# Narrow attention of layers two and three: maxima split and output normalised on GpSimd, masks one step ahead, query rows through DRAM

## The reference

```python
# layer two: positions and a mask
scores = jnp.einsum('bhqd,bhkd->bhqk', Q, K) * scale
scores = scores - slopes[None, :, None, None] * dist[:, None, :, :]
scores = jnp.where(mask[:, None, :, :] == 0, -jnp.inf, scores)
m = jnp.max(scores, axis=-1, keepdims=True)
e = jnp.exp(scores - m)
attn = e / (1.0 + jnp.sum(e, axis=-1, keepdims=True))
out = jnp.einsum('bhqk,bhkd->bhqd', attn, V)          # then @ W_o.T
# layer three: biases, a fixed mask and a key padding, plain softmax
energy = jnp.einsum('bhse,bhke->bhsk', qh, kh) * scale
energy = jnp.where(keep, energy, neg)
attn = jax.nn.softmax(energy, axis=-1)
x = x + jnp.tanh(g_xattn[n]) * attention(_layernorm(x), ctx, ctx, ...)
```

## Time and profile before

| | |
|---|---|
| median of 3 runs | 1532.38 us (1531.8 to 1533.9) |
| profiled execution | 1531.62 us, span 1529.8 us |
| busy: PE, PEld | 1339.7 us (88%), 743.4 us (49%) |
| busy: DVE, ACT, POOL | 1051.6 us (69%), 795.8 us (52%), 678.7 us (44%) |
| layer two attention | from 798.1 us to 1080 us of the span |
| layer three attention | from 1233.3 us to 1507 us of the span |

### The profile page before, as it was taken

The page is one execution under the profiler, slowest core; times in us unless marked ns, Lnnn a source line. Parts: engine busy times, 40 slices in busy tenths (PEclk is TensorE's granted clock), DMA queues, the critical chain, the costliest instruction groups (busy, mean ns, idle before and its releaser), DMA issues. The chain is left out here.

```text
span 1529.8 us, 32994 instructions
## 1 busy us (share of the span) xinstructions
PE 1339.7 (88%) x11860; PEld 743.4 (49%) x11868; DVE 1051.6 (69%) x3269; ACT 795.8 (52%) x1144; POOL 678.7 (44%) x542
## 2 busy tenths in 40 slices
PE   6999968748999999999746898999899859999994
PEld 4444454624666666666532333333577624333432
DVE  4988844166766666666478787686466778887876
ACT  2777723245656566565343555556433215655663
POOL 4766613514766676667524243230230073453310
PEclk8999978957999999999966999899799968999997
DMA  4566635446423442230034554330210032242301
GB/s 149 191 227 227 234 129 175 141 143 227 153 82 112 152 159 92 101 139 2 3 83 95 115 101 97 79 79 3 77 27 0 1 70 46 49 76 52 60 6 28
DMA packets 93029, 152.30 MB, mean 100 GB/s; under 512 B 18817, under 2 KB 64028, under 8 KB 89287
## 3 DMA queue, kind: packets, MB, share of 16 engines
q1 hardware_dynamic: 85312, 120.69, 28.0%
q10 hardware_dynamic: 2688, 25.56, 4.3%
q0 software_dynamic: 4880, 4.04, 1.2%
HBM read 93.66 MB, written 45.11 MB: 91 GB/s over the span
## 5 line engine op out<-in xcount | busy, mean ns | idle before, releaser
L1993 DVE CUSTOM_DVE_ANT_0 a_junk<-a_psM,a_madd 128x512 bf16<-128x512 f32 x512 | 331.4, 683 | 74.4 <-issue 69.3
L1936 ACT ACTIVATE a_probs<-a_psE 128x1024 f32<-128x1024 f32 x256 | 261.9, 1023 | 164.0 <-PE a_psE L1813 162.3
L2402 DVE TENSOR_REDUCE a_mx<-a_psM 128x1 f32<-128x512 f32 x236 | 148.2, 669 | 124.5 <-PE a_psM L2226 124.5
L1781 PE MATMUL a_psM<-narrow_k_op,narrow_q_op 57*64 57x512 bf16 (+1 forms) x1024 | 169.1, 423 | 33.6 <-DVE a_mx L1993 21.8
L2363 ACT ACTIVATE a_probs<-a_psE 128x1024 f32<-128x1024 f32 x128 | 130.8, 1024 | 85.9 <-PE a_psE L2248 82.6
L1639 POOL DMA_DIRECT2D narrow_q_op<-a_max_parts x96 | 50.3, 529 | 268.1 <-DVE a_max_parts L2006 268.0
L1825 PE MATMUL a_psO<-a_probs,narrow_values 128*32 128x256 f32 x2048 | 165.6, 398 | 1.8 <-ACT a_probs L1936 1.1
L2196 POOL TENSOR_TENSOR a_half_sum<-a_probs 128x1024 f32<-128x1024 f32 x64 | 150.7, 2355 | 32.8 <-ACT a_probs L2363 32.8
L2244 PE MATMUL a_psE<-a_qT,a_kT 64*128 64x256 f32 x1024 | 134.1, 382 | 0.0
L2260 PE MATMUL a_psO<-a_probs,a_values 128*64 128x256 f32 x1024 | 124.7, 386 | 0.8 <-ACT a_o_raw L2347 0.8
L2384 DVE RECIPROCAL a_o_raw<-a_o_raw 128x256 f32<-128x256 f32 x64 | 111.4, 1741 | 11.0 <-ACT a_o_raw L2347 11.0
(11 more groups left out here) (381 smaller groups left out, 2602.8 us busy)
## 6 DMA issues: line engine op xcount, KB each, us to landing
wide_k<-a_k_stage SPq DMA_DIRECT2D x32, 512.0 KB, 2.6
a_k_part<-wide_k SPq DMA_DIRECT2D x64, 256.0 KB, 3.2
wide_v<-a_v_stage SPq DMA_DIRECT2D x24, 512.0 KB
a_kT<-wide_k ACTq DMA_DIRECT2D x6, 2048.0 KB, 7.9
a_values<-wide_v ACTq DMA_DIRECT2D x6, 2048.0 KB
keys<-a_parts SPq DMA_DIRECT2D x96, 64.0 KB, 2.0
narrow_k_op<-keys SPq DMA_DIRECT2D x30, 192.0 KB
narrow_q_op<-a_y_parts SPq DMA_DIRECT2D x180, 32.0 KB
```

The source lines that it names most:

```text
L1781: last = pe.matmul(psM[j][c * n:(c + 1) * n, :], q_op[r][group, s // 2, s % 2 * P + c * n:s % 2 * P + (c + 1) * n], k_op[r][group, s // 2, :],
L1936: act.activation(probs[:, head:head + 2, k:k + 2, :], psE[es % 2][:], ACT.Exp).then_inc(exped, 1)
L1993: dve.tensor_tensor_reduce(junk[j][:], psM[j][:], madd[r][:, t, :], 1.0, -3.0e38, ALU.add, ALU.max, mx[r][:, max_place(h, t):max_place(h, ...
L2402: dve.tensor_reduce(mx[r][:, at:at + 1], max_bank(2 * p + t, j, first), AX.X, ALU.max).then_inc(max_read, 1)
```

## The change

- **Maxima.** ACT negates the turned maxima into SBUF (`negate`, after slots 8 and 0), POOL splits them there in four instructions and issues its own three DMAs right behind. DVE no longer does it.
- **Normalising.** ACT copies the turned outputs to SBUF (`T`, slot 2); DVE takes only the sums and reciprocals (slot 3); POOL multiplies. Turning back and projecting move to slots 5 and 7.
- **Masks.** The two masks are loaded and made separately, each before it is needed: the turned mask of batch v+1 between the two splits of step v, the other mask of batch v+2 after the second. The bias of layer three is added two tiles a step.
- **Query rows.** Chunks 1 to 3 and the second half of chunk 0 are stored to DRAM in six DMAs each (18 from ACT, 6 from SP), and a batch is loaded with two DMAs instead of twelve. POOL splits chunks 1 to 3.
- **Batch 0 first.** The first projection is cut in two halves of 256 columns; DVE splits these two alone, and SP issues the row copies as each part is ready.
- **Banks.** In step 0 the maxima of the first 12 slots rotate over three pairs of banks (`psM` and the four of `psE`); the first score waits until all of these are read.
- **Slopes.** One cast on POOL instead of four on ACT, in the phase before.

```diff
-        sp.wait_ge(self.slopes_cut, 4)
+        sp.wait_ge(self.slopes_cut, 1)
+        pool.tensor_copy(self.slopes_b[:], self.slopes[:]).then_inc(self.slopes_cut, 1)
...
-        MAX_SLOTS, READ_SLOT, OUT_SLOT, BACK_SLOT, PROJECT_SLOT, V_SLOT = (8, 0), 0, 2, 4, 6, 11
+        MAX_SLOTS, READ_SLOT, OUT_SLOT, INVERT_SLOT, BACK_SLOT, PROJECT_SLOT, V_SLOT = (8, 0), 0, 2, 3, 5, 7, 11
+        def max_bank(s, j, first):
+            i = s % M_SETS if first and s < LAG - 1 else 0
+            return psM[j][:] if i == 0 else psE[i - 1][:, j].rearrange("p k q -> p (k q)")
...
+        def store_queries(eng, n):
+            some = slice(2 * n, 2 * n + 2) if n else slice(1, 2)
+            for part in range(len(RUNS)):
+                for c in range(*RUNS[part]):
+                    eng.dma_start(q_scr[some, c].rearrange("b n q -> n b q"),
+                                  y_parts[n][:, part, (0 if n else S):].rearrange("p (b q) -> p b q", q=S)).then_inc(q_stored[n], 16)
...
             @block.sync
+                load_mask(0)
+                first_rows(sp, 0)
+                load_context(0)
...
+                for v in range(B):
+                    if 1 <= v < B - 1:
+                        if v >= 2:
+                            sp.wait_ge(exped, (v - 1) * HEADS)
+                        load_keys(v + 1)
+                        load_queries(v + 1)
+                        load_context(v + 1)
+                    maxima(v, 0)
+                    if v + 2 < B:
+                        if v >= 1:
+                            sp.wait_ge(masked, v)
+                            sp.wait_ge(masked_T, v)
+                        load_mask(v + 2)
+                        load_maskT(v + 2)
+                    if v + 1 < B:
+                        cross_masks(v + 1)
+                    maxima(v, 1)
             @block.gpsimd
+                def split_max(v, half):
+                    done = (2 * v + half) * n_split
+                    pool.wait_ge(max_negated, 2 * v + half + 1)
...
+                    split_three(pool, max_neg[half][:], [max_parts[half][:, k, :] for k in range(3)], max_rest[:], done, max_split)
+                    pool.wait_ge(max_split, done + n_split)
+                    maxima_rows(pool, v % RING, half, 1, max_in_other)
+                own_masks(0)
+                for n in range(1, NCHUNK):
+                    split_queries(n)
+                turned_masks(0)
+                own_masks(1)
                 for v in range(B):
+                    split_max(v, 0)
+                    if v + 1 < B:
+                        turned_masks(v + 1)
+                    if cfg.q_bias:
+                        bias_batch(v)
+                    split_max(v, 1)
+                    if v >= 1:
+                        normalise(v - 1)
                     if v + 2 < B:
+                        own_masks(v + 2)
+                normalise(B - 1)
             @block.scalar
+                for n in range(NCHUNK + 1):
                     act.wait_ge(query_made, n + 1)
+                    act.activation(tos[n], froms[n], ACT.Identity, bias=bqs[:] if cfg.q_bias else 0.0, scale=cfg.scale).then_inc(biased, 1)
+                    if n == 1:
+                        first_rows(act, 1)
+                for n in range(1, NCHUNK):
+                    act.wait_ge(split, 4 * n)
+                    store_queries(act, n)
...
+                        if after_first and s == MAX_SLOTS[1]:
+                            negate(v - 1, 1, inner or v >= 2)
+                        if finish:
+                            if s == OUT_SLOT:
+                                copy_turned(v - 2)
...
+                        if take_max and s == MAX_SLOTS[0]:
+                            negate(v, 0, inner or v >= 1)
             @block.vector
+                def invert(u):
+                    dve.wait_ge(turned_out, u + 1)
+                    sums = T[:].rearrange("p (n j m) -> p n j m", n=4, j=4)[:, :, :, HEAD_E:2 * SLOT:SLOT]
+                    dve.tensor_scalar(den[:], sums, cfg.sink, None, ALU.add).then_inc(den_done, 1)
+                    dve.wait_ge(den_done, u + 1)
+                    dve.reciprocal(rec[:], den[:]).then_inc(rec_done, 1)
```

More of the change, by code:

```diff
@@ L1735, in _ @@
                     if v + 2 < B:
-                        masks(v + 2, (v + 2) % RING, (v + 2) // RING, v + 2 < RING)
+                        own_masks(v + 2)
+                normalise(B - 1)
             @block.tensor
             def _(pe):
-                for n in range(NCHUNK):
-                    if n >= 2:
-                        pe.wait_ge(biased, n - 1)
-                    pe.matmul(psM[n % 2][:], wq[:], res.xnT[:, n * CHUNK:(n + 1) * CHUNK], start=True, stop=True).then_inc(query_made, 1)
@@ L1744, in _ @@
-                if cfg.q_bias:
-                    pe.matmul(psX[0:1, 0:D], nb.bv[:], wo[:], start=True, stop=True).then_inc(bias_made, 1)
-                pe.wait_ge(biased, NCHUNK)
-                if cfg.q_bias:
+                banks = [psE[0][:, 0, 0], psE[0][:, 1, 0], psE[1][:, 0], psE[1][:, 1], psO]
+                for n, bank in enumerate(banks):
+                    if n < 2:
+                        pe.matmul(bank, wq[:], res.xnT[:, n * S:(n + 1) * S], start=True, stop=True).then_inc(query_made, 1)
+                    else:
+                        pe.matmul(bank[:].rearrange("p k q -> p (k q)"), wq[:], res.xnT[:, (n - 1) * CHUNK:n * CHUNK], start=True, stop=True).then_inc(query_made, 1)
+                    if n == 1 and cfg.q_bias:
+                        pe.matmul(psX[0:1, 0:D], nb.bv[:], wo[:], start=True, stop=True).then_inc(bias_made, 1)
@@ L1773, in maximum @@
                 def maximum(v, r, s, j, first):
-                    n = QT * s + j
-                    if not (first and n < 2):
-                        pe.wait_ge(max_read, v * HEADS * QT + n - 1)
+                    back = M_SETS if first and s < LAG else 1
+                    if not (first and s < M_SETS):
+                        pe.wait_ge(max_read, v * HEADS * QT + QT * (s - back) + j + 1)
+                    elif s == 1 and j == 0:
+                        pe.wait_ge(biased, NCHUNK + 1)
                     group = slice(j * GROUP_ROWS, j * GROUP_ROWS + rows)
@@ L2656, in _ @@
                 norm.scalar(act, 1)
-                ahead.scalar(act, 2)
                 norm.copy(act, 1)
```

275 lines of the change are left out of this document (136 added, 139 removed).

## The result

| | before | after |
|---|---|---|
| median (10 runs each) | 1532.87 us (1531.38 to 1540.21) | 1523.54 us (1517.33 to 1525.79) |
| profiled execution, span | 1531.62 us, 1529.8 us | 1525.43 us, 1523.7 us |
| ratio | | 0.9925 [0.9909, 0.9942] |

Faster by 0.75%: the medians differ by 9.3 us, the ratio gives 11.5 (8.9 to 13.9). The forecast was a gain of 24 us and a time of 1508. 1523.5 lies inside the wide range, 1496 to 1525, but outside the forecast's own, 1500 to 1516, and less than half of the gain came. The two profiles, cut at the same places, and a second profile of the changed kernel (the first experiment) say where. Each number is the length of the stretch less its length before; the forecast's 1.5 us for the clock are split between the two starts.

The account below looks back on a forecast made before the run. TensorE and DVE were taken to hold each other through one pair of banks. The terms summed to -24.0 from 1531.6 us, with 0.8 added for the median: 1508 us; own range 1500 to 1516, 8-in-10 range 1496 to 1525.

Parts of the forecast that it names:

- the clock: At both attention layers' first scores, TensorE's 1.2 GHz level lasts somewhat longer after idling: +1.5 us for both.
- Slopes: Before layer two, POOL's cast hides in its idle time and the seam after ACT's end shrinks: -4.2 us.
- Start of layer two: Phase begin to first score: ACT's 18 stores and constants delay the first negation, rows landing at 36.1 us: +2.2 us.
- A steady step: Six full steps in each attention layer: less DVE work shortens TensorE's bank waits, 1.1 us a step, -13.2 us.
- the normalising: In each steady step, DVE's normalising falls from 1.0 to 0.6 us, counted as a gain of 0.1 us.
- Layer three: Layer three from first score to last add: forecast to shorten by 4.9 us.
- Step 1: Step 1 of each attention layer, with splits only, gains 0.7 us: -1.4 us in all.
- POOL in time: Steady steps: POOL's split takes 1.65 us and the second half's rows land 1.1 us before slot 5 needs them.
- Masks: Layer two: masks one step ahead remove the four waits for maxima rows and the layer's excess: -11.1 us.
- Start of layer three: Up to layer three's first score: POOL's masks and splits come last, rows landing at 34.3 us: -2.6 us.
- Tails: End of each attention layer: uncovered last-batch normalising costs 1.3 us and step 8 costs 1.1; +4.8 us for both layers.
- the first rival: Maxima rows take 1 us longer through POOL, ACT and landings, slot 5 waits in most steps: 1522 us, chance 0.16.

Follow-up runs that it names:

- the first experiment: The changed kernel with no edit, profiled a second time: 1518.13 us, ratio 0.9924 to the kernel before.
- before_slopes: The kernel before with one edit, the slopes cast in one piece on POOL: 1525.95 us, ratio 0.9996 to the kernel before.
- slopes_act: The changed kernel with the slopes cast on ACT in four pieces again: 1519.55 us, ratio 0.9943 to the kernel before.
- norm_dve: The changed kernel with the two products of the normalising moved back from POOL to DVE: ratio 1.001 to the kernel before.
- sp_stores: The changed kernel with ACT's 18 query-row stores issued by SP, six in each of steps 0 to 2: 1504.44 us, ratio 0.9845 to the kernel before.
- split_dve: The changed kernel with the split of the maxima moved back to DVE: ratio 1.0029 to the kernel before.
- masks_late: The changed kernel with both masks made together behind the second split and loaded one step later: ratio 1.0104 to the kernel before.
- best1: The changed kernel with query stores on SP behind the second half's maxima, POOL's later splits moved into steps, slopes cast early on ACT: ratio 1.0028 to the kernel before.

## Why the prediction was half right

**Slopes: wrong.** The step named the work that would hide POOL's cast, "on a POOL that has finished the positions and waits for the norm". It asked whether POOL was free and not whom it disturbs. The seam gave its 4.4 us, the ternary phase took 3.3 to 3.6 back: -1 us, shown by before_slopes and slopes_act. The rule of the Trainium skill that is cited at norm_dve (SBUF — State Buffer, section Who interferes with whom) would have given this rival and was not weighed.

**Start of layer two: the term that failed.** "ACT's last six stores, at 0.6 each ... end at 24": all 18 took 1.15 each in the mean. The second six alone took 9.9 us, so the last six began at 25.9, not at 20, and ended at 32.7; the first negation came at 39.4 and the first score at 44.8, for 36. Stores had been priced one by one, from the 64 KB stores of the earlier trace rows and from the maxima rows, as if the price did not depend on what is under way; here twelve row copies, two masks, keys and 24 stores fall into one stretch, with a DMA share of 0.96 and more. Even the bound of 1 us each (+8) was too low. That the stores ahead of ACT's other work made the start late is shown by sp_stores: the same 18 stores on SP, spread over three steps, bring the first score forward by 12.7 us, and 0.49 us each is then near the price forecast.

**A steady step: right.** 28.12 us for 28.2. split_dve shows that the split's share is real and mostly smaller than DVE's time: 0.6 to 1.5 us a step for two splits of 1.1, 1.0 forecast. The waits that the rule speaks of are gone: 31 and 25 waits for a bank before, two and two after. The 0.1 us for the normalising was too little: undone, it costs 0.5 in layer two and 1.5 in layer three, most of the latter by DVE and POOL in each other's way, so the two parts are not additive.

**Layer three, -6.7 for -4.9: partly luck.** The step at the loop's turn fell from 32.8 to 29.7 us, 3.1 where 1.1 was counted, and the prediction did not know of it. Step 1 gained nothing (34.7 us from first score to the first copy, before and after), where 0.7 was counted.

**POOL in time: right.** The split is 1.63 us, and the waits for rows have gone but for 0.7 us in layer two and 1.2 in layer three.

**Masks: right in size, half right in cause.** -16.1 us in layer two for -16.0, where 11.1 were counted for layer two's excess; against before_slopes, which has half of the excess, it would be -10. But of the four waits of before only two had POOL's rows behind a mask (DVE's split ended at 946.89, POOL issued at 951.66). For the wait at 894.35 the split ended at 887.05, POOL issued at 887.34 and SP at 887.07, done at 889.13, and TensorE went on 5.2 us later, for a usual landing of 1.7. Which of the changes freed these (the masks, or the twelve copies per batch that are two loads now) was not taken apart. masks_late shows only that the new attention needs the new order.

**Start of layer three: right by luck** (-2.2 for -1.8 with the clock). The terms as written, mask to 5.2 and three splits of 4.0, give 17.2 and not "19.2"; with 17.2 the start would be -4.6, not -2.6. In the run the splits did end at 19.2, because POOL, done with the mask at 5.0, stood idle for 2.63 us until ACT's chunk was there, a wait that the prediction does not have. And POOL was not alone on the path: ACT's stores ended at 1264.95, POOL's masks at 1265.88. **Tails:** +4.8 forecast; 2 x 0.96 more of waiting for the products, and 0.2 and 1.2 us in step 8 of the layers (18.25 and 19.25 for 18.02 and 18.01), 3.4 in all.

The gap between -24 and the -12 of the second profile is these two terms: 8.5 us at the start of layer two, 3.4 in the ternary phase. The rest cancels: the other rows gained 3.4 us more than forecast, and the stretch ahead of the ternary phase, which comes and goes, cost 3.6. That the time lies in the wide range, near the 1522 of the first rival, is luck too: that rival's mechanism, late maxima rows in most steps, did not happen, and the loss came from two other terms.

## What to carry to other kernels

Work moved to an engine that waits is free only if it takes nothing that a busy engine uses: look at what DVE does beside each new POOL instruction, and in which memory its operands lie. A long row of DMA issues is priced by what is already under way in the stretch where it will stand, not by the row of one issue elsewhere; on an engine that has urgent work behind it, a long row of bulk stores belongs somewhere else (12.7 us here). Small urgent transfers want few loads issued ahead of them on the same engine.

## What the runs showed of the hardware

Issuing a 128 KB store took ACT 0.45 to 0.90 us for the first nine, and 3.4, 2.2 and 2.2 us for the next three, the first of which began when none of the nine had landed; the DMA share was 0.86 to 1.11 through all of this. Transfers of 2 KB took 1.7 us to land in the steady state; behind 3.3 MB of loads (best1) POOL's took 3.1 to 6.4 us, and TensorE went on 9.3 us after SP's last. The Trainium skill (DMA: Bandwidth & Descriptors, section Issuing engines are not separate DMA queues) says that all issuers run on the same 16 engines; the trace fits this, since SP's masks and loads were in flight when ACT's issues slowed. It adds that issuing from several engines saves only the time to initiate, usually small beside the DMA itself. That time was small for the 0.49 us on SP and not for the 1.15 on ACT, 20.75 us in all for the 18.

DVE's operations on SBUF were two to four times as long beside POOL's: 0.71 for 0.18 us, 1.01 for 0.49, 3.86 for 1.43.
